# A fused attention, top-k feed-forward and layer norm kernel: another order of the squares, the root and the state on GpSimd, VectorE and ScalarE

## The reference

```python
xn = (x - mean) / sqrt(var + 1e-5)

# attention: 16 heads of 32, chunks of 128 rows, per-head decay r
q, k, v = xn @ Wq, xn @ Wk, xn @ Wv          # q, k rotated (first 8 of 16 pairs turn)
for each chunk:                               # a state kv of 32 x 32 per head is carried
    inter  = (q * q_decay) @ kv
    intra  = ((q @ k.T) * decay_mask) @ v
    kv     = r**128 * kv + (k * k_decay).T @ v
attn = inter + intra
attn = attn * rsqrt(mean(attn**2) + 1e-5) * rms_w
a = attn @ Wo

# feed-forward: ternary weights, each row keeps its 204 largest of 2048 values
z = xn @ ternary(W_syn).T + b_syn
thresh = 204th largest value of the row
hidden = where(z >= thresh, relu(z), 0)
f = layernorm(xn + hidden @ ternary(W_out).T + b_out) * gamma + beta

out = x + a + f
```

## Time and profile before

| | |
|---|---|
| median of 3 runs (lowest, highest) | 970.13 us (969.19 to 970.22) |
| the profiled execution's own time | 972.45 us |
| its span | 970.7 us |
| PE busy | 910.7 us, 94% of the span |
| DVE busy | 794.7 us, 82% |
| POOL busy | 770.8 us, 79% |
| ACT busy | 697.6 us, 72% |
| mean granted TensorE clock | 0.984 of full speed |

### The profile page before, as it was taken

How to read it: one execution, slowest core, us unless ns; L and a number is a source line. 1 busy time by engine, 2 the same in 40 slices (tenths; PEclk the granted TensorE clock), 3 DMA queues, 4 the chain that set the end, 5 groups by cost and what they waited for, 6 DMA issues and landing times.

```text
span 970.7 us, 22604 instructions
## 1 busy us (share of the span) xinstructions
PE 910.7 (94%) x8467; PEld 437.7 (45%) x8467; DVE 794.7 (82%) x1925; ACT 697.6 (72%) x1289; POOL 770.8 (79%) x655
## 2 busy tenths in 40 slices
PE   5847999999999999999999999999999999999987
PEld 2423544444444444444444444444444444444434
DVE  5878878887888988878899887778988887798885
ACT  6788657777666787776677777777787767778662
POOL 1547697888798888888888888898887888988863
PEclk9968999999999999999999999999999999999989
DMA  9875634345343434445444365343444544434431
GB/s 331 256 181 98 110 70 80 72 99 99 77 99 69 86 76 89 99 87 89 84 71 83 82 99 99 77 99 66 89 77 88 99 82 95 84 70 94 82 71 40
DMA packets 257425, 94.52 MB, mean 97 GB/s; under 512 B 243488, under 2 KB 243744, under 8 KB 256544
## 3 DMA queue, kind: packets, MB, share of 16 engines
q1 hardware_dynamic: 253472, 85.64, 44.2%
q10 hardware_dynamic: 3840, 7.41, 2.1%
HBM read 24.34 MB, written 8.39 MB: 34 GB/s over the span
## 4 chain that ended last, share of the span: by engine, by line
PE 28%; POOL 27%; ACT 25%; issue 10%; DVE 5%; DMA 3%; SPq 1%; DVEq 0%; POOLq 0%; ACTq 0%
PE proj L1061 10%; PE p_ffn L1173 9%; PE p_ffn L1203 6%; ACT Pr L618 6%; POOL pair_c L792 4%; POOL xrn L780 4%; POOL area L795 4%; POOL xrn L781 4%; POOL xhl L775 3%; ACT Pr L609 3%; ACT kvs L508 2%; ACT dump_x L477 2%; ACT hl L627 2%; POOL pair_a L865 2%; ACT dump_x L473 2%
## 5 line engine op out<-in xcount | busy, mean ns | idle before, releaser
L1061 PE MATMUL proj<-wqkv,xT 128*128 128x512 f16 x1152 | 261.5, 384 | 0.6 <-DVE area L1455 0.6
L1061 PE MATMUL proj<-wsynT,xT 128*128 128x512 f16 x1024 | 246.7, 385 | 4.3 <-DMA wsynT<-xrn 3.0
L848 POOL TENSOR_TENSOR hl<-area,hl 128x2048 f16<-128x2048 f32 x31 | 139.2, 4490 | 62.4 <-ACT hl L627 62.4
L1061 PEld LDWEIGHTS proj<-wqkv,xT 128*128 128x128 f16 x1152 | 112.3, 99 | 134.5 <-issue 6.5
L1061 PEld LDWEIGHTS proj<-wsynT,xT 128*128 128x128 f16 x1024 | 93.4, 99 | 116.7 <-issue 14.5
L1173 PE MATMUL p_ffn<-woutT,area 128*128 128x512 f16 x480 | 111.5, 384 | 0.0
L550 ACT ACTIVATE area<-area 128x512 f16<-128x512 f32 x64 | 36.8, 622 | 100.5 <-POOL area L802 100.5
L1203 PE MATMUL p_ffn<-woutT,area 128*128 128x512 f16 x480 | 108.5, 379 | 0.0
L1562 DVE MAX8 cand<-area 128x8 f32<-128x128 f32 x512 | 107.6, 277 | 1.1
L1455 DVE SCALAR_TENSOR_TENSOR area<-proj,c,gb 128x512 f32<-128x512 f32 x128 | 92.5, 743 | 16.6 <-PE proj L1061 15.7
L1217 PE MATMUL p_wo<-wo,ahl 128*128 128x512 f16 x384 | 90.2, 384 | 4.1 <-ACT ahl L445 2.3
(11 more groups left out here) (249 smaller groups left out, 1785.7 us busy)
## 6 DMA issues: line engine op xcount, KB each, us to landing
xrn<-in_L_attn_x_dram SPq DMA_DIRECT2D x32, 256.0 KB, 3.0
out_dram<-pair_b SPq DMA_DIRECT2D x29, 256.0 KB, 2.1
woutT<-in_L_ffn_W_syn_dram ACTq DMA_DIRECT2D x2, 1024.0 KB, 10.8
area<-in_L_ffn_W_syn_dram ACTq DMA_DIRECT2D x2, 1024.0 KB, 11.9
woutT<-in_L_ffn_W_out_dram SPq DMA_DIRECT2D x2, 1024.0 KB, 6.6
area<-in_L_attn_Wq_dram ACTq DMA_DIRECT2D x1, 1024.0 KB, 7.3
area<-in_L_attn_Wk_dram ACTq DMA_DIRECT2D x1, 1024.0 KB, 9.6
area<-in_L_attn_Wv_dram ACTq DMA_DIRECT2D x1, 1024.0 KB, 11.8
```

The source lines that it names most:

```text
L848: nc.gpsimd.tensor_tensor(hl[:, 1, :], src, hl[:, 0, :], ALU.subtract).then_inc(S["lo_ready"], 1)
L1061: last = nc.tensor.matmul(bank, xT[:, b.par, k, :], w, start=m == 0, stop=m == len(pairs) - 1)
```

## The change

On GpSimd, from tile 2 on: `root_of_squares(t)` no longer opens the next step but stands between the two halves of `qk_low(b)` at the end of its own; `q_joined(t)` stands ahead of the vd product; `rotary(b)` ahead of the row norm's root, `out_root(d)` ahead of the biases; `rotary_added(b)` ahead of `squares_added(t)` in every such step. On VectorE, from tile 3 on: state and mean square ahead of the flags; `factors(u)` ahead of `threshold(u)` and `next_guess(u)`; `q_decayed(t)` ahead of `below(t)`; `segments(t, 2)` ahead of the probabilities; `z_chunk(b, 1)` inside the selection. On ScalarE, from tile 3 on, `diagonal(u)` stands ahead of the counts; from tile 2 on, `hidden_high(u)` ahead of `qkv_out(b, 0)`. On TensorE, `factors_spread(u)` stands ahead of the first projection.

```diff
@@ ScalarE, step @@
+                if t.n > 2:
+                    diagonal(u)
                 search_begun(t)
                 first_count(t)
                 guess_moved(t)
-                diagonal(u)
+                if t.n == 2:
+                    diagonal(u)
                 second_count(t)
                 guess_settled(t)
+                hidden_high(u, z[:, u.par, :])
                 qkv_out(b, 0)
-                hidden_high(u, z[:, u.par, :])
                 qkv_out(b, 1)
@@ GpSimd @@
-            def qk_low(b):
+            def qk_low(b, between=None):
                 for m in range(2):
+                    if m and between:
+                        between()
                     wait(pool, "qk_hi", b, 2, m + 1)
...
-                if u:
+                if u and u.n < 2:
                     root_of_squares(u)
+                if t.n > 1:
+                    q_joined(t)
...
-                if t.n > 0:
+                if t.n == 1:
                     q_joined(t)
...
+                if t.n > 1:
+                    rotary(b)
                 if a and t.n > 1:
                     wait(pool, "ln_stat", a, 4, 4)
                     power(r256, ve, "r256_ready")
+                if d:
+                    out_root(d)
                 if t.n > 1:
                     biases(b)
...
                 if a:
                     low_half(a)
-                if d:
-                    out_root(d)
...
                 if t.n > 1:
-                    rotary(b)
-                    if b.n == NT - 1:
-                        rotary_added(b)
+                    rotary_added(b)
                     squares_added(t)
-                    if b.n < NT - 1:
-                        rotary_added(b)
                 if d and b.n < NT - 1:
                     out_scaled(d)
                     out_added(d)
-                qk_low(b)
+                qk_low(b, (lambda: root_of_squares(t)) if t.n > 1 else None)
@@ TensorE, step @@
                 if b.n > 1:
+                    if t.n > 2:
+                        factors_spread(u)
                     for n in range(3):
                         projection(b, n)
-                        if n == 0:
+                        if n == 0 and t.n <= 2:
                             factors_spread(u)
@@ VectorE, step @@
                 z_chunk(t, 3)
+                if t.n > 2:
+                    state_moved(u)
+                    mean_square(u)
                 flags(u, p_wo[0:1, 0:1])
-                state_moved(u)
-                mean_square(u)
+                if t.n <= 2:
+                    state_moved(u)
+                    mean_square(u)
+                if t.n > 2:
+                    factors(u)
                 threshold(u)
                 next_guess(u)
-                factors(u)
+                if t.n <= 2:
+                    factors(u)
                 hidden(u, z[:, u.par, :])
...
                 attention_normalised(u)
+                q_decayed(t)
                 below(t)
                 segments(t, 0)
                 segments(t, 1)
-                q_decayed(t)
+                segments(t, 2)
                 probs(t, 0)
...
                 z_chunk(b, 0)
-                segments(t, 2)
-                z_chunk(b, 1)
+                segments(t, 3)
                 attention_added(u)
-                segments(t, 3)
-                selection(t)
+                selection(t, lambda: z_chunk(b, 1))
                 z_chunk(b, 2)
```

5 lines of the change are left out of this document (2 added, 3 removed).

## The result

| | before | after |
|---|---|---|
| median (lowest, highest) | 970.17 us (969.19 to 972.43) | 990.34 us (989.64 to 990.92) |
| span of the profiled execution | 970.7 us | 988.5 us |

The changed kernel takes 1.0204 times as long, 95% interval 1.0185 to 1.0223. The forecast was 979, with 970 to 988 as its range: the direction was right, the loss was 20 us where 9 had been forecast, and it lies outside the range.

What follows compares the result with a forecast made beforehand. PE bound the kernel, needing 27.60 us of each 28.01 us step. A new ring through GpSimd's root summed to 28.33, 0.32 longer in some 27 steps: 8.7 us on 970.13, said as 979, range 970 to 988.

Steps and rivals of the forecast that it cites:

- The ring: Loop between first counts through ScalarE's counts, VectorE's `below`, GpSimd's work and root, VectorE's factors and guess: 28.33 us, without PE.
- points 1 and 2: ScalarE from first count to settled guess, 5.51 us; then VectorE starts `below` 0.05 later, which takes 2.34.
- point 3: GpSimd's `hidden_low` can't overlap `below` and ends 3.94 us after it; the high half being ready earlier is worth nothing.
- point 4: GpSimd's `attention_low` falls from 1.60 to 1.16 us, 1.08 without overlap, since `q_decayed` is moved; gains 0.45.
- point 5: GpSimd's small work: row norm's root 0.52, biases 2.46, low half of x to output's sum 9.35; together 12.33 us.
- point 6: One half of q and k's low part on GpSimd, 1.13 us, then root to VectorE's first factor, 0.57.
- The guess beside the second subtraction: VectorE's guess falls 0.1 us before GpSimd's second subtraction ends; a wait of 0 to 0.1 possible, taken as 0.
- the rule taken to the end of the row: VectorE instruction with two SBUF inputs and GpSimd one shut each other out throughout: guess waits 0.1, sum 28.43 us.
- the two kinds of row: VectorE's guess before the change: 1.17 us if starting 0.01 after GpSimd's subtraction, 0.16 if starting 0.01 before it.
- Point 7: VectorE's first factor to third 0.25 us, from there to the guess 0.74, then guess to ScalarE's first count 0.39.
- (c): Rival: low half's DMA lands later and lengthens the ring by 0.5 us a step, 992 us; chance above 985: 0.12.
- (b): Rival: ring drops under PE's 27.60 us, root done before the flags arrive, gaining 11 us: 959; chance below 968: 0.12.

Runs made afterwards that it cites:

- the first experiment: Changed kernel with the factors (VectorE) back behind the next guess and the diagonal (ScalarE) behind the moved guess: 969.79 us, ratio 0.9944 to the kernel before.
- the first experiment's kernel with the longer GpSimd work: The kernel of the first experiment with one more GpSimd operation of about 0.5 us in each step: 971.59 us, ratio 0.9998 to the kernel before.

## Why the prediction was right in direction and wrong in size

**What held.** The ring is the cause: undoing the factors and the diagonal takes it away, adding 0.52 us to GpSimd adds 0.54 to the step, and moving TensorE's waits about wins nothing. Point by point, the rows around 605.93 give: points 1 and 2 5.53 and 0.04 (5.51 and 0.05 said), `below` 2.35, point 3 3.94 as said, with `hidden_low` starting before `below`'s end, point 4 1.08 as said, the small work of point 5 from 590.36 to 602.68 12.32 (12.33 said), point 6 1.12 and 0.58 (1.13 and 0.57 said), the guess to the count 0.39. The guess beside the second subtraction took 0.16 at 605.54, no more: this one ran from 604.32 to 605.48. It had just ended, since the guess came 0.17 later than the forecast had it. Two other kernels decide between the 0 that I took and the 0.1 set beside it. With the third factor behind the guess, the guess starts 0.18 ahead of the subtraction's end and is 0.03 longer. In the first experiment's kernel with the longer GpSimd work it meets the first subtraction later in its course (timeline of DVE, then POOL):

```profile
620.34 0.47 DVE L1613 SCALAR_TENSOR_TENSOR c<-c 128x1 f32<-128x1 f32 x1
...
619.64 1.15 POOL L809 TENSOR_TENSOR area<-area 128x512 f16<-128x512 f32 x1
```

It starts 0.45 ahead of that row's end and ends 0.02 behind it; less its own 0.16 it could go on 0.14 ahead of that end. So a guess that starts in the last 0.1 waits for nothing: the 0 was right, and the rule taken to the end of the row adds 0.1 that isn't there. Two smaller points: the high half's move isn't worth nothing, as point 3 has it, but 0.13 us a step (the experiment with q's copy first); and the two kinds of row that the forecast tells apart by 0.01 us are not told apart by the printed starts alone: in the kernel before, a guess at 761.80, 0.01 behind the subtraction, took 0.16, and one at 369.63, 0.01 ahead of it, 1.18. VectorE's wait for the root is 1.40 us, TensorE left the chain, and it waits where the forecast said.

**Where it failed**, in the order of size:

1. **Point 7 was mis-sized.** From the first factor to the guess it is 605.54 - 604.38 = 1.16, not 0.25 + 0.74 = 0.99. The 0.74 came from the mean square to the guess. I took it for the price from any last instruction to the guess. But the guess didn't hang on the mean square there: the threshold's register load had begun at 621.22, behind the flags and 0.16 ahead of the mean square's start, and ran beside it. What has a fixed price is the way from the load's start to the guess, 0.90 in both kernels. In the changed one the load starts only with the third factor, 0.26 behind the first, and 0.26 + 0.90 = 1.16. With it the quiet step is 28.51 and not 28.33: 0.18 x 27 = 4.9 us. The third factor's move to behind the guess let the load start with the first factor, and gave 0.22 back. My list of uncertain terms held nothing on it.
2. **A quiet step was set against a mean.** 28.33 was the sum for a step in which nothing is late; 28.01 was the mean over all of before. Against before's quiet step of 27.86 the same sum gives 0.47 a step, 12.7 us and not 8.7. The change takes away the meetings of guess and subtraction, but not the other lateness. The mean after lies 28.62 - 28.51 = 0.11 above its quiet step: 3.0 us. VectorE's longer idle time at the threshold's branch (0.81 for 0.44 at 662.69) makes five steps of 28.81 to 28.89, about 1.7 of the 3.0; the longest step, 29.16 from 262.39 on, isn't one of them, and its cause isn't shown. Before's mean at the first counts was 27.99, not 28.01: another 0.5.
3. **The basis of the sum.** The sum was worked out against the profiled execution of before, 972.45, and then put on the median 970.13, "the difference applies to all alike". It doesn't: after's profiled execution, 990.33, is at its median, while 972.45 lay 2.2 above the highest of before's three. Before's steps turn on which of two instructions comes first by 0.01 us, so its executions can differ; that this makes the 2.3 isn't shown, since only one of them has a trace. The changed kernel, whose guess no longer meets the subtraction, was better put at 972.45 plus its own steps. For the same reason the 20 us themselves are uncertain by some: beside the experiments before's median was 971.8 to 974.3, and the kernel with the transpose ahead, whose steps are the changed kernel's, took 989.9 on the chip where before took 974.3. The loss may be nearer 16 to 19 us; the changed kernel wasn't run there, so this stays open.
4. Entry and exit, taken as nothing within 1.5, cost 1.6 at the first and gave 1.0 back at the last step and the tail: 0.6.

Together 8.7 + 4.9 + 3.0 + 0.5 + 0.6 = 17.7, against the span's 17.8; and with the 2.3 of the basis, 20.0 against 20.2.

**The rivals.** (c), the low half's DMA, would have been the one that gives 992, and the time alone would have spoken for it. The transpose's move shows that it isn't: 989.9 us, in quiet steps of 28.51. (b) named a real kernel under a wrong condition. The ring does get under TensorE's floor as soon as it no longer holds the guess; the floor itself, which I had at 27.60 by taking away the one wait shown, is 27.33, so its price was too low: (28.01 - 27.33) x 27 = 18 us and not 11. The change with the factors behind the guess doesn't reach it by itself (0.6%); 954 us against 974 took the transpose's move and the other form of the guess as well.

**What stays open.** What makes VectorE idle for some 0.35 us longer at its branch in some steps was not tried. In the kernel before with the other form of the guess such steps are 28.19 long with one of 27.52 behind, so that the two together lose nothing (twice 27.86 is 55.72, their sum 55.71); in the changed kernel 28.88 is followed by 28.52, and nothing is given back.

## What to carry to other kernels

Before an instruction that waits is moved ahead of one that others wait for, write down the ring that this closes, and set its quiet step against the quiet step of now, each with its own lateness on top. Here one wait of three small instructions, ahead of the guess or behind it, decided between 990 and 970 us. A price read from one place (mean square to guess) must be taken apart before it is used at another: what in it ran beside something there? Here it was the register load, which the chain of waits prints cut down to what nothing else covers; its own row has its start.

## What the runs showed of the hardware

- The threshold's register load on VectorE takes 0.30 to 0.31 us (changed kernel, nearly all steps), and the guess stands 0.90 us behind its start, unless VectorE is idle for longer at the branch. The load doesn't wait for the end of the instructions ahead of it: it starts 0.01 us behind the start of the third factor, 0.02 behind that of the first with the third moved away, and before the mean square in the kernel before (621.22 against 621.38).
- A VectorE instruction on one column with two SBUF tensors took 0.16 us, or, started while a GpSimd subtraction ran, until 0.01 to 0.02 us behind the end of the subtraction's row: 0.95 when it started 0.94 ahead of that end (first experiment, 368.18), 0.47 at 0.45 ahead, 0.19 at 0.18 ahead. The form with one tensor and a column as its scalar took 0.21 in 29 of 29. The Trainium skill, SBUF — State Buffer, section Who interferes with whom, says that a VectorE instruction with at most one SBUF input, outside its two-port modes, doesn't contend with GpSimd; these rows agree, if the column scalar isn't counted as an input.
- TensorE's quiet step is 27.33 us in three kernels, 0.27 less than the step of before without its one shown wait. Where that rest lay isn't shown.
